# Rotary scores from two products: half of the query groups are no longer summed on VectorE, and the five engines' lists of a tile are reordered

## What is computed

```python
b, s, _ = x.shape                                   # after a layer norm of x
qkv = jnp.einsum('bsh,oh->bso', x, w_qkv)           # H, HKV, D = 16, 4, 128
q, k, v = jnp.split(qkv, [H * D, (H + HKV) * D], axis=-1)
q = _layernorm(q, qn_g, qn_b); k = _layernorm(k, kn_g, kn_b)   # per head
q = q * cos + _rotate_half(q) * sin
k = k * cos + _rotate_half(k) * sin
scores = jnp.einsum('bhqd,bhkd->bhqk', q, jnp.repeat(k, rep, axis=1)) / jnp.sqrt(D)
weights = jax.nn.softmax(jnp.where(causal, -jnp.inf, scores), axis=-1)
attn = jnp.einsum('bhqk,bhkd->bhqd', weights, jnp.repeat(v, rep, axis=1))
return jnp.einsum('bsd,od->bso', attn.transpose(0, 2, 1, 3).reshape(b, s, H * D), w_o)
```

## Time and profile before

| | us |
|---|---|
| runs of the kernel before | 3070.69 to 3077.81, median 3075.42 |
| profiled execution, device time | 3078.19 |
| its span, first to last instruction | 3076.4 |
| busy, whole span: TensorE, VectorE, ScalarE, GpSimd | 2646.2, 2017.7, 1573.7, 1405.2 |

### The profile page before, as it was taken

The page is one execution under the profiler, slowest core; times in us unless marked ns, Lnnn a source line. Parts: engine busy times, 40 slices in busy tenths (PEclk is TensorE's granted clock), DMA queues, the critical chain, the costliest instruction groups (busy, mean ns, idle before and its releaser), DMA issues. The chain is left out here.

```text
span 3076.4 us, 86672 instructions
## 1 busy us (share of the span) xinstructions
PE 2646.2 (86%) x33275; PEld 1934.0 (63%) x33291; DVE 2017.7 (66%) x3674; ACT 1573.7 (51%) x2950; POOL 1405.2 (46%) x1522
## 2 busy tenths in 40 slices
PE   3888888888876888886779989999999999999576
PEld 2677777777751222222468867888888888888333
DVE  5888888888866788884878862343434343433697
ACT  3565555556544677772134433444444444444587
POOL 4888888888852223322434421222222222222487
PEclk9999999999996899997989989999999999999899
DMA  3000000000002232320011110000000000000000
GB/s 125 2 0 0 0 0 0 0 0 0 0 1 86 83 94 86 91 82 11 0 39 31 34 52 31 7 4 4 5 3 5 3 5 3 5 32 1 4 24 27
DMA packets 94668, 75.60 MB, mean 25 GB/s; under 512 B 17520, under 2 KB 88560, under 8 KB 93424
## 3 DMA queue, kind: packets, MB, share of 16 engines
q1 hardware_dynamic: 94576, 74.35, 7.9%
HBM read 55.97 MB, written 17.04 MB: 24 GB/s over the span
## 5 line engine op out<-in xcount | busy, mean ns | idle before, releaser
L1394 DVE TENSOR_REDUCE x_mx<-x_ps 128x2 f16<-128x512 f32 x512 | 332.8, 683 | 57.2 <-PE x_ps L1458 54.3
L1363 ACT ACTIVATE x_e<-x_ps 128x512 f32<-128x512 f32 x512 | 292.2, 596 | 55.1 <-PE x_ps L1462 38.1
L361 POOL TENSOR_TENSOR x1s<-x1s,x1mx 128x1024 f32<-128x1024 f32 x32 | 60.8, 1900 | 519.0 <-DVE x1mx L357 519.0
L1458 PE MATMUL x_ps<-x_k,x_q 32*128 32x256 f16 x1024 | 199.4, 292 | 80.9 <-ACT x_e L1363 48.0
L1722 ACT ACTIVATE x_q<-x_ps,x_q_bias,x_q_scale 128x128 f32<-128x128 f32 x512 | 185.7, 467 | 159.7 <-PE x_ps L105 159.7
L1458 PEld LDWEIGHTS x_ps<-x_k,x_q 32*128 32x128 f16 x1024 | 58.1, 93 | 269.4 <-DVE x_mx L1394 130.4
L431 ACT CAST x1oh<-x_ps 128x1024 f16<-128x1024 f32 x64 | 64.7, 1012 | 313.0 <-PE x_ps L423 313.0
L103 PE MATMUL a_ps<-ln_xha,a_wq 128*128 128x128 f16 x1024 | 180.3, 222 | 51.2 <-ACT a0v L678 44.0
L627 POOL TENSOR_TENSOR a_w<-a_qsw,a_tab 128x512 f32<-128x512 f32 x128 | 176.6, 1380 | 57.3 <-ACT a_qsw L688 56.0
L1462 PE MATMUL x_ps<-x_q,x_k 32*128 32x256 f16 x1024 | 201.0, 293 | 1.7 <-ACT x_e L1363 1.4
L280 DVE TENSOR_TENSOR ln_xlx<-x_ps,ln_xhx 128x256 f16<-128x256 f32 x32 | 13.6, 424 | 281.6 <-ACT x_xt L1714 281.6
(11 more groups left out here) (369 smaller groups left out, 9144.1 us busy)
## 6 DMA issues: line engine op xcount, KB each, us to landing
x_q<-x_q_rows SPq DMA_DIRECT2D x32, 256.0 KB, 2.8
x_k<-x_k_rows SPq DMA_DIRECT2D x32, 256.0 KB, 3.1
a_stage<-in_x_w SPq DMA_DIRECT2D x32, 256.0 KB, 2.6
x_vt<-in_ctx_v SPq DMA_DIRECT2D x32, 144.0 KB, 2.3
stage<-in_x_wt SPq DMA_DIRECT2D x4, 1028.0 KB, 6.4
x_all<-in_x SPq DMA_DIRECT2D x8, 512.0 KB, 10.0
x_cf<-in_ctx SPq DMA_DIRECT2D x32, 128.0 KB, 2.1
x_q_rows<-x_xhl SPq DMA_DIRECT2D x32, 128.0 KB, 1.7
```

Source lines behind the costliest of these rows:

```text
L1363: act.activation(e[:, u % ES].rearrange("p c n -> p (c n)"), s2_ps(u), ACT.Exp, scale=XT ** -0.5).then_inc(e_ready, 1)
L1394: dve.reduce_max(mx[:, p % 2, c:c + 2], s1_ps(u), AX).then_inc(mx_ready, 1)
L1458: return pe.matmul(s1_ps(u)[:, c], q[r, p % 4, g, c * P:(c + 1) * P], k[r, p % 4, g], start=True, stop=True)
```

## The change

In `scores`, the heads of query groups 0 and 1 (`JOINED = 2`) keep one product, of u + w. For groups 2 and 3 the addition on VectorE is left out, and two products, u with the keys and w with the keys, are summed in the PSUM bank. The semaphores for u and u + w become one for each group, since the groups are no longer done in order. `square` is split into the squares and `swap_query`, and `keys_summed` into `keys_summed` and `keys_joined`. All five lists of a step get a new order: on TensorE `bias_scores` comes first and `value` after `query_sums`, `at_.values` 1 ahead of `at_.project` 0; on ScalarE the swap of group 0 comes first, `value` and `at_.high` 1 ahead of the exponential, the swap of group 3 last; on GpSimd the squares go ahead of w for groups 2 and 3; on VectorE the order of the groups is 1, 2, 0, 3, with 0 and 3 and both additions at the end of the list.

```diff
 X_PIECE = 4
+JOINED = 2
 
...
         k_ready, vp_ready, q_ready, ksum_ready = (sem(n) for n in ("k_ready", "vp_ready", "q_ready", "ksum_ready"))
-        ksw_ready, qsw_ready, u_ready, w_ready = (sem(n) for n in ("ksw_ready", "qsw_ready", "u_ready", "w_ready"))
+        ksw_ready, qsw_ready, w_ready = (sem(n) for n in ("ksw_ready", "qsw_ready", "w_ready"))
+        u_ready = [sem(f"u_ready{g}") for g in range(4)]
         sqh_ready, sql_ready = sem("sqh_ready"), sem("sql_ready")
-        sqk_ready, sq_ready, uw_ready = sem("sqk_ready"), sem("sq_ready"), sem("uw_ready")
+        sqk_ready, sq_ready = sem("sqk_ready"), sem("sq_ready")
+        uw_ready = [sem(f"uw_ready{g}") for g in range(JOINED)]
         kraw_ready, vk_ready, rkd_ready, rkb_ready, kt_ready = (sem(n) for n in ("kraw_ready", "vk_ready", "rkd_ready", "rkb_ready", "kt_ready"))
...
                 pool.wait_ge(qsw_ready, 4 * t + g + 1)
-                wait_used(pool, uw_ready, t, 1, 4, g + 1)
+                if g < JOINED:
+                    wait_used(pool, uw_ready[g], t, 1)
+                else:
+                    wait_used(pool, at_.sc_ready, t, 1)
                 pool.tensor_tensor(by_head(w, g), by_head(qsw, g), table(QW), ALU.mult).then_inc(w_ready, 1)
...
                     squares_low(t + 1, 1)
+                    squares_low(t + 1, 2)
                 at_.normalise(pool, t)
                 if has_next:
-                    for g in (2, 3):
-                        swapped_part(t + 1, g)
-                        squares_low(t + 1, g)
+                    squares_low(t + 1, 3)
+                    swapped_part(t + 1, 2)
+                    swapped_part(t + 1, 3)
             over_tiles(pool, head, step)
...
                 act.activation(by_head(sqh, g), heads_of(ps[:, QBANK[g], :]), ACT.Square).then_inc(sqh_ready, 1)
+
+            def swap_query(t, g):
+                act.wait_ge(q_ready, 4 * t + g + 1)
                 wait_used(act, w_ready, t, 1, 4, g + 1)
...
                     square(0, g)
+                    swap_query(0, g)
                 ln.high(act, 1, 1, q_ready, 4)
...
                 if has_next:
+                    swap_query(t + 1, 0)
                     square(t + 1, 0)
-                if has_next:
                     square(t + 1, 1)
-                at_.exponential(act, t)
-                if has_next:
-                    value(t + 1, 1 - p)
+                    swap_query(t + 1, 1)
                 if before:
...
                 if has_next:
+                    value(t + 1, 1 - p)
+                at_.exponential(act, t)
+                if has_next:
                     square(t + 1, 2)
+                    swap_query(t + 1, 2)
                     square(t + 1, 3)
...
                     ln.high(act, t + 2, p, q_ready, 4)
+                if has_next:
+                    swap_query(t + 1, 3)
             over_tiles(act, head, step)
...
 
-            def keys_summed(t, p):
+            def keys_summed(t):
 
...
                 dve.tensor_scalar(vk[:, :], ps[:, 0, 0:KV], 1.0 / HD, LN_EPS * WS * WS, ALU.mult, ALU.add).then_inc(vk_ready, 1)
+
+            def keys_joined(t, p):
+
                 dve.wait_ge(kraw_ready, t + 1)
...
                 dve.wait_ge(qsw_ready, 4 * t + g + 1)
+                dve.wait_ge(sqh_ready, 4 * t + g + 1)
                 wait_used(dve, at_.sc_ready, t, 1)
-                dve.tensor_tensor(by_head(u, g), heads_of(ps[:, QBANK[g], :]), table(QC), ALU.mult).then_inc(u_ready, 1)
+                dve.tensor_tensor(by_head(u, g), heads_of(ps[:, QBANK[g], :]), table(QC), ALU.mult).then_inc(u_ready[g], 1)
 
             def add_swapped(t, g):
-                dve.wait_ge(u_ready, 4 * t + g + 1)
+                dve.wait_ge(u_ready[g], t + 1)
                 dve.wait_ge(w_ready, 4 * t + g + 1)
-                dve.tensor_tensor(by_head(u, g), by_head(u, g), by_head(w, g), ALU.add).then_inc(uw_ready, 1)
+                dve.tensor_tensor(by_head(u, g), by_head(u, g), by_head(w, g), ALU.add).then_inc(uw_ready[g], 1)
 
...
                 keys_raw(0, 0)
-                keys_summed(0, 0)
+                keys_summed(0)
+                keys_joined(0, 0)
                 rotate_query(0, 0)
...
                 ln.low(dve, 1, 1)
-                for g in range(4):
+                for g in range(JOINED):
                     add_swapped(0, g)
...
                 before = not (isinstance(t, int) and t == 0)
-                if has_next:
-                    keys_raw(t + 1, 1 - p)
                 dve.wait_ge(var_ready, t + 1)
...
                 if has_next:
-                    keys_summed(t + 1, 1 - p)
+                    keys_raw(t + 1, 1 - p)
+                    keys_summed(t + 1)
                 dve.wait_ge(s2_ready, t + 1)
...
                     ln.stats(dve, ch, t + 2, p)
+                if has_next:
+                    keys_joined(t + 1, 1 - p)
                 dve.wait_ge(at_.sc_ready, t + 1)
...
                 if has_next:
-                    rotate_query(t + 1, 0)
                     keys_scaled(t + 1, 1 - p)
                     rotate_query(t + 1, 1)
-                    add_swapped(t + 1, 0)
-                at_.denominator(dve, ch, t)
-                if before:
-                    at_.low(dve, t - 1, 1, not has_next)
                 if further(t):
                     ln.normalise(dve, t + 2, p)
+                if before:
+                    at_.low(dve, t - 1, 1, not has_next)
+                at_.denominator(dve, ch, t)
                 if has_next:
                     rotate_query(t + 1, 2)
-                    add_swapped(t + 1, 1)
-                    rotate_query(t + 1, 3)
                 if before:
...
                 if has_next:
-                    add_swapped(t + 1, 2)
-                    add_swapped(t + 1, 3)
+                    rotate_query(t + 1, 0)
+                    add_swapped(t + 1, 1)
+                    rotate_query(t + 1, 3)
+                    add_swapped(t + 1, 0)
             over_tiles(dve, head, step)
...
                 pe.wait_ge(ln.xl_ready, t + 1)
-                wait_used(pe, u_ready, t, 1, 4, 2)
+                wait_used(pe, u_ready[1], t, 1)
                 for h in range(KV):
...
             def value(t, p):
-                wait_used(pe, u_ready, t, 1, 4, 4)
+                wait_used(pe, u_ready[3], t, 1)
                 for c in range(KC):
...
                 if g == 0:
-                    wait_used(pe, u_ready, t, 1, 4, 1)
+                    wait_used(pe, u_ready[0], t, 1)
                 elif g == 1:
...
             def scores(t, p):
-                pe.wait_ge(uw_ready, 4 * (t + 1))
+                for g in range(4):
+                    pe.wait_ge(uw_ready[g] if g < JOINED else u_ready[g], t + 1)
+                pe.wait_ge(w_ready, 4 * (t + 1))
                 if not (isinstance(t, int) and t == 0):
...
                         for h in range(2):
-                            last = pe.matmul(at_.sc[h * SEQ:(h + 1) * SEQ, 2 * k + b, :], u[:, b, 2 * k + h, :],
-                                             kt[:, p, first_key:first_key + SEQ], start=True, stop=True)
+                            to = at_.sc[h * SEQ:(h + 1) * SEQ, 2 * k + b, :]
+                            keys_of = kt[:, p, first_key:first_key + SEQ]
+                            joined = k < 2 * JOINED
+                            last = pe.matmul(to, u[:, b, 2 * k + h, :], keys_of, start=True, stop=joined)
+                            if not joined:
+                                last = pe.matmul(to, w[:, b, 2 * k + h, :], keys_of, start=False, stop=True)
                 last.then_inc(at_.sc_ready, 1)
...
 
-                pe.wait_ge(u_ready, 4 * (t - 1) + 3)
+                pe.wait_ge(u_ready[2], t)
                 ln.transpose(pe, t, p)
...
                 before = not (isinstance(t, int) and t == 0)
+                bias_scores(t, p)
                 if has_next:
                     keys(t + 1, 1 - p)
-                    value(t + 1, 1 - p)
                 if before:
...
                 query_sums(t)
-                bias_scores(t, p)
                 if has_next:
+                    value(t + 1, 1 - p)
                     key_sums(t + 1)
...
                     key_factors(t + 1)
-                if before and has_next:
-                    at_.project(pe, t - 1, 0)
-                    at_.values(pe, t - 1, 1 - p, 1)
-                elif before:
-                    at_.values(pe, t - 1, 1 - p, 1, True)
+                if before:
+                    at_.values(pe, t - 1, 1 - p, 1, not has_next)
                     at_.project(pe, t - 1, 0)
```

More of the change, by code:

```diff
@@ L818, in step @@
                 if has_next:
-                    rotate_query(t + 1, 0)
                     keys_scaled(t + 1, 1 - p)
                     rotate_query(t + 1, 1)
-                    add_swapped(t + 1, 0)
-                at_.denominator(dve, ch, t)
+                if further(t):
+                    ln.normalise(dve, t + 2, p)
```

(5 more changed lines are left out.)

## The result

The changed kernel takes 2970.41 us in the median of 4 runs (2966.28 to 2981.61) against 3074.76 for the kernel before, measured beside it; the ratio is 0.9667, with a 95% interval of 0.9638 to 0.9697. Beside each other a second time the two gave 0.9663 (0.9643 to 0.9684). The forecast was 2984, in a range of 2970 to 3030; the median lies 0.4 us inside the lower end of it. The profiled execution took 2968.17, with a span of 2966.3.

The account below looks back on a forecast made before the run. It took a ring of waits as the bound, no engine being full. TensorE's work plus 0.2 to 0.3, with 0.1 for waits, cut the tile from 26.38 to 23.4, 91.4 us in all: 2984, range 2970 to 3030.

Parts of the forecast that it names:

- Scores: TensorE's scores: a second product for groups 2 and 3 adds 32 passes at 31.6 ns, +1.01 us a tile.
- Rivals B: TensorE's scores: the weight load paces the added passes at 53 ns, +0.7 us a tile, 3006 us; chance 0.05.
- D: TensorE's scores: accumulating into the same addresses stalls it, 222 ns a pass, a tile of 29.3 us, 3166; chance 0.05.
- Bias product: TensorE: 0.94 us of bias product moves into the gap before `keys`, so the scores can start at 5.2.
- Scores taken up and maximum: VectorE takes the scores at 8.34 us after `keys` starts (before 8.27); maximum ready at 13.47 (before 13.40).
- The two edits: TensorE: longer scores (+1.01 us) and the bias product moved ahead of `keys` (0.94 us) cancel for the maximum's time.
- Swap 0: ScalarE's swap ahead of squares 0: `swapped_part` 0 starts at 12.1 instead of 13.13, the subtraction 1.03 us earlier.
- Exponential: ScalarE: value and `at_.high` 1 fill its wait, the exponential starts at 16.85, TensorE's 1.52 us gap before queries 3 goes.
- u2: VectorE's step for group 2, needed by TensorE's transposes of the next rows: ready at 21.1 us, slack 0.8.
- GpSimd's list: GpSimd's steps after the subtraction: six of 1.38 us, one at most 2.35, ending 4.1 into the next tile, hidden.
- Rival A: A ring over GpSimd takes over because w3 releases the scores: tile 24.0 to 25.4 us, 3029 in all; chance 0.25.
- two additions fewer: VectorE: 2.9 us of its work a tile goes; worth little by itself since VectorE is not full, but makes room.

Follow-up runs that it names:

- e4: The changed kernel with no group joined: no additions, two products for every group; tile 24.19 us, ratio 0.9778 to the kernel before.
- e1: The changed kernel's new order with all four groups joined by additions on VectorE, two more at its list's end; tile 23.29 us, ratio 0.9672.

## Why the prediction was right, and where it was off

The forecast's case came, by its own steps: the tile is 23.19 in the mean and 23.27 in the middle of the stage, for the 23.4 of the sum. Counted from `keys` at 508.70:

- *Scores*: 516.90 - 513.91 = 2.99 us for the 96 passes and the step to the values, forecast 3.03. The first 36 passes lie at (515.01 - 513.91) / 36 = 30.6 ns, the next 56, of which half accumulate, at (516.64 - 515.01) / 56 = 29.1. Rivals B (53 ns) and D (222 ns) are out; e4 gives 31 ns again.
- *Bias product*: with the 0.94 of the earlier trace rows it is over at 508.56, and `keys` starts 0.14 later. Forecast 0.2 to 0.3.
- *Scores taken up and maximum*: 8.37 and 13.34, forecast 8.34 and 13.47. The two edits do cancel.
- *Swap 0*: `swapped_part` 0 at 12.07, the subtraction 14.42 to 16.77; forecast 12.1, 14.45 and 16.8.
- *Exponential*: 16.80 for 16.85, and no gap before queries 3 and project 1.
- *u2*: 20.52 to 21.2 for 21.1. The next `keys` at 23.27.
- *GpSimd's list*: w3 ends 3.2 us into the next tile, for the 4.1 I allowed. The bound of 2.35 for a step of 1.90 was too careful, and the additions that are gone stretch nothing. Rival A never came near: the scores need w3 only at 5.2. Two additions remain in VectorE's tail and took 1.63 and 1.16, for 1.3 each.

The signs that it named came too: the subtraction starts 523.12 - 517.07 = 6.05 us behind L830 for 6.1, and 64 additions are left of 128.

Where it was off: the 0.1 us that I put on the wait instructions isn't there, and the gap before `keys` is 0.14. The steady 23.27 is the 23.3 that stood before that addition. In the stage the 31 intervals gave 98.7 us and its end 2.5 more, less 1.0 at its start, where the first tile's longer scores were put at 0: 100.2 for 91.4. That is 8.8 of the miss of 13.6 in the median. The rest lies in stages to which the forecast gave 0: the profiled execution gained 13.7 in one, with a higher clock, and lost 4.5 in another, to pauses of TensorE. The range allowed for neither. Its lower end, 2970, was TensorE's bare work and nothing for other stages, so that the median of 2970.41 lies inside it is partly luck; the second median, 2968.69, does not.

One reading in it was weak: it priced "two additions fewer" as what makes room in VectorE's tail. The room wasn't needed (e1: 23.29 with all four). Further additions at the end of the list run in GpSimd's pause at 0.79 us, not at the 1.3 that I took from the earlier trace rows. The forecast held because its sum rested on TensorE's work, which the products only raise. It gave no figure for the order alone, and that was nearly all of it.

## What to carry to other kernels

When several engines are each near 85% and none is full, add up the work of each between its waits first: the largest sum (22.0 here, against 26.4) is what reordering alone cannot go under. It need not get there: with the order alone it was 23.29, as another engine came next. Experiments with one move undone at a time give the price of each move. A trade of work between engines pays only up to the crossing: here one group in four on TensorE, three on VectorE. A gain in one stage must be read in that stage: a clock that returns sooner or later and code that is loaded again moved single stages by 6 to 16 us, as much as the last improvement was worth (15.4).

## What the runs showed of the hardware

- Changing only how many products TensorE's code has in one stage changed the time of a later loop in which not a line differs: 923 us with none or four groups joined, 925 to 929 with two, 939 with three. The slow ones move 128 instruction packets in that stage for 16; the slowest have up to 22 pauses of up to 1.4 us, the changed kernel 9 of up to 0.6. Adding 286 small products at the program's start brought 939 back to 923.
- The same fp32 addition of two 128x512 tiles in SBUF on VectorE takes 0.79 us (three in 2.36, the first 0.6 us of them beside GpSimd) while GpSimd pauses, and 1.15 each (3.44 for three) or 1.79 beside it.
- An accumulating fp32 pass of 64 columns onto the addresses that the pass before it wrote costs 29 to 31 ns, as much as one onto new addresses.
- An untouched stage took 412 to 433 us, in step with the clock granted over it, 0.94 to 0.84; the same code differed by 6 us and by 12.5 us between two runs.
